# Transposed token buffers laid out by batch, with the third token tile as two 64-column stationary operands

## The chip, the cores and the metric

The kernel runs on one core of one Trainium2 chip. Its time is device microseconds of that core: before the change 1238.06 us, the median of 3 runs (1237.32 to 1239.3). The engines are PE (TensorE, with its weight loads shown as PEld), DVE (VectorE), ACT (ScalarE), POOL (GpSimd) and SP (SyncE, which issues most of the DMAs). They run side by side and meet at semaphores only.

## The reference, cut to what matters

Sixteen images of 112 x 112 become 49 image tokens each (convolutions and a wavelet branch, then a layer norm); a class token is put ahead and 128 text tokens behind, so each batch entry has T = 178 tokens of width D = 192. Then come an attention layer over 12 heads of 16, and a layer with a second attention (its logits are normalised) and a mixture of 4 experts:

```python
h = concat([tok(x), txt], axis=1)                        # (16, 178, 192)
h = h + attn(layernorm(h), w_qkv, b_qkv, scale, w_proj, b_proj)   # diagonal of the non-class part masked
# ffn(layernorm(h)), added to h:
logits = gamma * zscore_last(q @ k.T * hd ** -0.5)
x = layernorm(src + softmax(logits) @ v @ Wo.T + bo)
gate_scores = softmax(x @ Wg.T + bg)                     # 4 experts, the two best are kept
h1 = relu(einsum('btd,edf->ebtf', x, W1) + b1)           # 192 -> 768, for each expert
y = einsum('ebtf,efd->ebtd', h1, W2) + b2                # 768 -> 192
out = layernorm(x + einsum('ebtd,bte->btd', y, combine))
```

## The kernel before, in words

After a stage that makes the image tokens (up to about 160 us), the batch is worked off in 8 pairs of two entries, 356 tokens a pair. With **tokens in the partitions** a pair has three tiles of 128 rows: the text of entry 0, the text of entry 1, and a third tile whose rows 0 to 49 are the image and class tokens of entry 0 and rows 64 to 113 those of entry 1. With **tokens in the columns** (the transposed buffers `xT`, `x2T_hi`, `x2T_lo`, `osb`, `oT`, `hid` and their PSUM banks) a buffer has XW = 384 columns in the same order: 128 of text, 128 of text, 64 of images, 64 of images. So a tile is always one run of 128 columns (`tile_cols`, L593), and whoever works through all tokens takes XN = 370 columns, of which 356 hold tokens.

Each pair goes through attention twice (s = 0 and 1) and then through the experts. A round of the program handles three pairs at a time: the first attention of pair a, the second of pair b, the experts of pair m. Everything is ordered by hand: each engine has its own program, and the expert work is cut into 50 steps a pair which are put between the attention's steps by the tables FILL, FILL_A7 and FILL_B7 (so many steps at each named point). Even steps are `MoePe.step` of unit u (24 units: 4 experts x 6 slices of 128): five matmuls with w1 stationary and the tokens moving (L655), which split a float32 product into float32r parts. Odd steps are `second` (L677): the slice's hidden values `hid` are stationary, one 128-column tile at a time, and w2's 192 columns move. So on PE L655 and L677 take turns. The first rounds have no expert work; there `pe_warm` (L751) puts dummy matmuls between. The last round has expert work alone.

What else the change touches on PE: `pe_project` (L776) makes queries and keys for all tokens at once; `pe_tokens` (L784) makes values and output projections, with each tile of tokens stationary; `pe_out` (L879) turns the attention's result `osb` back, three 128 x 128 transposes for each tile; `bias` (L665) adds the experts' biases with `combT` stationary; the gate's scores (L999) are four small matmuls a tile. The logits (`pe_logits`, L811, L817, L826) aren't changed, but L817 already works with halves of 64 columns that land in the upper and lower partitions, and so does L503 in the image stage.

On ACT the copies of queries, keys, `mrows` and `osb` (L1054 to L1098) are each two instructions, one for the text columns and one for the image columns, since their destination is ordered by batch. On DVE `dve_front1` centres the tokens in two pieces, and `dve_gate` (L1392, L1393) adds up the gate's scores.

Of the kernel before, what the change touches and what calls it, by code (L numbers as in the profile page):

```python
# [29 lines left out]
ALU = mybir.AluOpType  # L30
ACT = mybir.ActivationFunctionType
# [3 lines left out]
HC = D // 2  # L35
# [25 lines left out]
XN = 2 * NTXT + 64 + NB  # L61
# [23 lines left out]
CHAIN_STEPS = {"dve_tok": 15, "dve_front0": 19, "dve_front1": 10, "dve_norm1": 13, "dve_split": 8, "dve_max0": 8, "dve_max1": 8,  # L85
# [50 lines left out]
def build(nc, a):  # L136
    ctx = ExitStack()
    with ctx:
# [391 lines left out]
        xbar = sb("xbar", [HC, 2, 2, 2])  # L530
# [54 lines left out]
        def text(t):  # L585

            return t[:, :, 0:2 * NTXT].rearrange("p h (b j) -> p h b j", b=2)

        def images(t, n=NB):

            return t[:, :, 2 * NTXT:XW].rearrange("p h (b j) -> p h b j", b=2)[:, :, :, 0:n]

        def tile_cols(t, half, i):  # L593

            return t[:, half, 128 * i:128 * i + 128]
# [37 lines left out]
        class MoePe(Moe):  # L633


            def step(self, u, odd):
# [6 lines left out]
                elif u == UNITS:  # L643
                    pe.wait_ge(S["comb_ready"], at(m, 1, 1))
                    for i in range(3):
                        ins = nc.tensor.transpose(PS[0:E, 4, 128 * i:128 * i + 128], comb[:, i, :], ident[:])
                    ins.then_inc(S["ct_psum"], 1)
                    self.second(UNITS - 1)
                else:
# [9 lines left out]
            def bias(self):  # L659
# [4 lines left out]
                for i in range(3):  # L664
                    ins = nc.tensor.matmul(tile_psum((6, 7), i), combT[:, 128 * i:128 * i + 128], b2[:],  # L665
                                           start=(i != 1), stop=True, skip_group_check=True)
                ins.then_inc(S["bias_psum"], 1)

            def second(self, u):
# [5 lines left out]
                for i in range(3):  # L675

                    ins = nc.tensor.matmul(tile_psum((6, 7), i), hid[u % 2][:, 128 * i:128 * i + 128], w2[:, u, :],  # L677
                                           start=(j == 0 and i != 1), stop=(j == FT - 1), skip_group_check=True)
                ins.then_inc(S["h_used"], 1)

        class MoeAct(Moe):


            def step(self, u, odd):
                act, m = self.eng, self.m
                if not odd and u < UNITS:
# [3 lines left out]
                    nc.scalar.activation(hid[u % 2][:, 0:XN], PS[:, 4 + u % 2, 0:XN], ACT.Relu,  # L690
                                         bias=b1[:, u:u + 1]).then_inc(S["h_ready"], 1)
                elif not odd:
                    act.wait_ge(S["ct_psum"], at(m, 1, 1))
                    nc.scalar.copy(combT[:, 0:XN], PS[0:E, 4, 0:XN]).then_inc(S["ct_ready"], 1)
# [68 lines left out]
        def pe_turn_in(pe, s, r):  # L763

            pe.wait_ge(S["xn_ready", s], at(r, 1, 1))
            for h in range(2):
                for i in range(3):
                    ins = nc.tensor.transpose(PS[0:HC, front(s, r)[h], 128 * i:128 * i + 128], xn[s][:, i, HC * h:HC * h + HC],
# [3 lines left out]
        def pe_project(pe, banks, w, x, done):  # L772

            for m in range(2):
                for k in range(2):
                    ins = nc.tensor.matmul(PS[0:HC, banks[m], 0:XN], w_at[:, w, k, HC * m:HC * m + HC], x[:, k, 0:XN],  # L776
# [3 lines left out]
        def pe_tokens(banks, w, x, done):  # L780

            for i in range(3):
                for k in range(2):
# [994 lines left out]
```

## Time and profile before

| | us |
|---|---|
| median of 3 runs | 1238.06 |
| the profiled execution | 1242.59 |
| its span | 1240.8 |
| PE busy | 1114.1 (90%) |
| PE weight loads busy | 816.6 (66%) |
| DVE busy | 680.4 (55%) |
| ACT busy | 397.6 (32%) |
| mean granted TensorE clock | 0.94 |

Busy time of PE is from modelled ends of matmuls that overlap, so the start of one matmul to the start of the next is the surer measure of what one costs. A float32 matmul is two instructions in the profile. A row of the timeline joins like instructions that follow one another: the number behind x is how many, the second column is the time from the first one's start to the last one's end.

### The profile page before, as it was taken

The numbers are of one execution on the slowest core, as the hardware profiler recorded it, in microseconds if no ns is written. First come the engines' busy times: TensorE is split into PE (matmuls) and PEld (weight loads), VectorE is DVE, ScalarE is ACT, GpSimd is POOL, SyncE is SP. The second block draws the span as 40 slices with busy tenths as digits, with TensorE's granted clock in tenths as the row PEclk, the third lists the DMA queues.
The fourth block names the chain that finished last, engine by engine and source line by source line (L and its number), as shares of the span: only waits on it lengthen the run. The fifth ranks groups of instructions, "written<-read, shape, count | busy, mean of one in ns | idle before, by whom it ended". The sixth has DMA issues, their size and how long they took to land.

```text
span 1240.8 us, 19314 instructions
## 1 busy us (share of the span) xinstructions
PE 1114.1 (90%) x7726; PEld 816.6 (66%) x7726; DVE 680.4 (55%) x1874; ACT 397.6 (32%) x905; POOL 55.6 (4%) x90
## 2 busy tenths in 40 slices
PE   7898887898889999999999999999999989888895
PEld 4343354554577678667866785688578757676795
DVE  3357777454555566556646564665557653643432
ACT  1223221322323343324243334334343333232321
POOL 6001110000000000000000000000000000000000
PEclk9898897999989899989998999899999998898998
DMA  9000034412042104310530152024203320040000
GB/s 307 1 1 0 1 125 82 88 43 46 8 86 66 29 5 106 63 18 10 111 63 9 28 111 45 9 49 90 45 9 73 66 45 2 1 88 8 1 10 9
DMA packets 38481, 60.79 MB, mean 49 GB/s; under 512 B 5060, under 2 KB 30264, under 8 KB 37944
## 3 DMA queue, kind: packets, MB, share of 16 engines
q1 hardware_dynamic: 36112, 56.84, 21.4%
q10 hardware_dynamic: 2280, 2.72, 0.8%
q8 instruction: 61, 1.00, 0.3%
q14 instruction: 28, 0.23, 0.1%
HBM read 42.76 MB, written 16.34 MB: 48 GB/s over the span
## 4 chain that ended last, share of the span: by engine, by line
PE 62%; DVE 15%; ACT 4%; DMA 3%; issue 2%; SPq 1%; POOL 0%; DVEq 0%; ACTq 0%; POOLq 0%
PE PS L677 15%; PE PS L655 12%; DVE mx L1349 7%; PE PS L776 6%; PE PS L870 5%; PE PS L811 5%; PE PS L784 5%; PE PS L817 3%; PE PS L879 2%; PE PS L826 2%; DMA qst<-mrows 1%; PE PS L908 1%; PE PS L999 1%; DVE acc L705 1%; ACT probs L1087 1%
## 5 line engine op out<-in xcount | busy, mean ns | idle before, releaser
L677 PE MATMUL PS<-w,hid 128*128 128x192 f32 x1152 | 233.1, 340 | 2.6 <-DVE acc L705 1.9
L690 ACT ACTIVATE hid<-PS,b 128x370 f32<-128x370 f32 x192 | 109.3, 569 | 321.7 <-PE PS L655 320.1
L677 PEld LDWEIGHTS PS<-w,hid 128*128 128x128 f32 x1152 | 199.1, 198 | 13.5 <-issue 4.8
L1349 DVE TENSOR_REDUCE mx<-PS 128x2 f32<-128x356 f32 x288 | 128.8, 521 | 130.8 <-PE PS L811 100.6
L1087 ACT ACTIVATE probs<-PS 128x356 f32<-128x356 f32 x288 | 110.8, 484 | 21.9 <-PE PS L811 12.4
L655 PE MATMUL PS<-x2T_hi,w_hi 128*128 128x370 f32 x192 | 91.2, 475 | 0.0
L811 PE MATMUL PS<-kst,qst 96*128 96x178 bf16 x384 | 66.6, 269 | 12.8 <-DMA kst<-scr_k 5.5
L826 PE MATMUL PS<-masks,ident_bf 128*128 128x256 bf16 (+1 forms) x288 | 75.4, 262 | 0.0
L870 PE MATMUL PS<-probs,va 128*17 128x178 f32 x1536 | 67.3, 315 | 6.4 <-ACT probs L1087 6.4
L776 PE MATMUL PS<-xT,w_at 96*96 96x370 f32 x192 | 67.1, 493 | 2.9 <-ACT xT L1047 2.0
L655 PE MATMUL PS<-x2T_lo,w_hi 128*128 128x370 f32 x192 | 66.0, 344 | 0.0
L655 PE MATMUL PS<-x2T_hi,w_lo 128*128 128x370 f32 x192 | 65.9, 343 | 0.0
L655 PE MATMUL PS<-x2T_hi,w_rest 128*128 128x370 f32 x192 | 65.8, 343 | 0.0
L655 PE MATMUL PS<-x2T_lo,w_rest 128*128 128x370 f32 x192 | 65.7, 342 | 0.0
L811 PE MATMUL PS<-qst,kst 99*128 99x178 bf16 x384 | 54.5, 243 | 9.7 <-DMA qst<-mrows 6.1
L751 PE MATMUL PS<-masks,ident_bf 128*128 128x356 bf16 x322 | 57.0, 324 | 4.0 <-POOL hid L1674 4.0
L1370 DVE RECIPROCAL rs<-PS 128x36 f32<-128x36 f32 x16 | 6.1, 383 | 97.5 <-PE PS L879 97.5
L811 PEld LDWEIGHTS PS<-kst,qst 96*128 96x128 bf16 x384 | 26.4, 103 | 44.4 <-DVE mx L1349 28.3
L870 PEld LDWEIGHTS PS<-probs,va 128*17 128x17 f32 x1536 | 39.9, 97 | 22.6 <-ACT probs L1087 9.2
L384 DVE SCALAR_TENSOR_TENSOR dwo<-pad_l,chan,dwo 96x441 f32<-96x441 f32 x48 | 38.0, 792 | 27.5 <-ACT cw L308 26.0
L776 PEld LDWEIGHTS PS<-xT,w_at 96*96 96x96 f32 x192 | 30.7, 167 | 30.6 <-ACT xT L1047 5.6
L705 DVE SCALAR_TENSOR_TENSOR acc<-PS,comb,acc 128x192 f32<-128x192 f32 x72 | 25.6, 411 | 43.0 <-PE PS L677 43.0
(228 smaller groups left out, 1760.9 us busy)
## 6 DMA issues: line engine op xcount, KB each, us to landing
qst<-scr_q SPq DMA_DIRECT2D x96, 144.0 KB, 4.8
scr_q<-qs SPq DMA_DIRECT2D x16, 432.0 KB, 3.3
scr_k<-ks SPq DMA_DIRECT2D x16, 432.0 KB, 3.3
kst<-scr_k SPq DMA_DIRECT2D x16, 432.0 KB, 5.0
kst<-scr_k SPq DMA_DIRECT2D x16, 288.0 KB, 5.9
cols<-in_x_cols SPq DMA_DIRECT2D x6, 392.0 KB, 10.0
w<-in_w SPq DMA_DIRECT2D x1, 2304.0 KB, 26.2
kst<-scr_k SPq DMA_DIRECT2D x16, 144.0 KB, 6.3
```

The lines of the kernel that those rows point to most:

```text
L655: ins = nc.tensor.matmul(PS[:, 4 + u % 2, 0:XN], w[:, f], x[:, plane, 0:XN], start=(k == 0), stop=(k == 4))
L677: ins = nc.tensor.matmul(tile_psum((6, 7), i), hid[u % 2][:, 128 * i:128 * i + 128], w2[:, u, :], start=(j == 0 and i != 1), stop=(j == FT ...
L690: nc.scalar.activation(hid[u % 2][:, 0:XN], PS[:, 4 + u % 2, 0:XN], ACT.Relu, bias=b1[:, u:u + 1]).then_inc(S["h_ready"], 1)
L705: ins = nc.vector.scalar_tensor_tensor(out=acc[:, i, :], in0=tile_psum((6, 7), i), scalar=comb[:, i, e:e + 1], in1=(acc if e else x2)[:, i ...
L751: nc.tensor.matmul(PS[:, 7, 0:T2], ident_bf[:], masks[:], start=True, stop=True)
L776: ins = nc.tensor.matmul(PS[0:HC, banks[m], 0:XN], w_at[:, w, k, HC * m:HC * m + HC], x[:, k, 0:XN], start=(k == 0), stop=(k == 1))
L784: ins = nc.tensor.matmul(tile_psum(banks, i), tile_cols(x, k, i), w_at[:, w, k, :], start=(k == 0), stop=(k == 1))
L811: ins = nc.tensor.matmul(PS[:, bank, T * b:T * b + T], still[0:rows_, h, TP * b:TP * b + NTXT], move[0:rows_, h, TP * b:TP * b + T], start ...
L826: ins = nc.tensor.matmul(own, ident_bf[:], m.rearrange("p (b j) -> p b j", b=2), start=False, stop=True, skip_group_check=True)
L870: ins = nc.tensor.matmul(PS[32 * q:32 * q + VW, 3, T * b:T * b + T], va[s][:, 2 * i + b, h, :], pr, start=(i == 0), stop=(i == 1), skip_gr ...
L1087: nc.scalar.activation(probs[:, u % PROB_UNITS, bank, :], PS[:, bank, 0:T2], ACT.Exp)\
L1349: nc.vector.tensor_reduce(out, PS[:, g, 0:T2].rearrange("p (b j) -> p b j", b=2), AX.X, ALU.max)\
```

## The change

All buffers with tokens in the columns now hold 192 columns for each of the two entries: 128 of text, 50 of images and class, 14 unused. Work on all tokens takes 2 x 178 = 356 columns in two runs (`by_batch`). The two text tiles are still 128 columns in one run, but the third tile is 64 columns at 128 and 64 columns at 320. As a moving operand or as output of a transpose that is one access of 2 x 64 (`tile_of`). As a stationary operand it is two (`lhs_of`), each of 64 columns, whose results go to partitions 0 to 63 and 64 to 127.

```diff
-XN = 2 * NTXT + 64 + NB
+GATE_COLS = (0, 192, 128, 256)
...
+        def by_batch(t, n=T):
+            return t.rearrange("p (b j) -> p b j", b=2)[:, :, 0:n]
...
+        def lhs_of(t, i):
+            if i < 2:
+                return ((t[:, TP * i:TP * i + NTXT], slice(0, 128)),)
+            return tuple((t[:, TP * b + NTXT:TP * b + TP], slice(64 * b, 64 * b + 64)) for b in range(2))
...
-                        ins = nc.tensor.matmul(PS[:, 4 + u % 2, 0:XN], w[:, f], x[:, plane, 0:XN],
+                        ins = nc.tensor.matmul(by_batch(PS[:, 4 + u % 2, 0:XW]), w[:, f], by_batch(x[:, plane, :]),
                                                start=(k == 0), stop=(k == 4))
...
                 for i in range(3):
-                    ins = nc.tensor.matmul(tile_psum((6, 7), i), hid[u % 2][:, 128 * i:128 * i + 128], w2[:, u, :],
-                                           start=(j == 0 and i != 1), stop=(j == FT - 1), skip_group_check=True)
+                    for lhs, rows_ in lhs_of(hid[u % 2][:], i):
+                        ins = nc.tensor.matmul(tile_psum((6, 7), i)[rows_], lhs, w2[:, u, :],
+                                               start=(j == 0 and i != 1), stop=(j == FT - 1), skip_group_check=True)
...
         def pe_tokens(banks, w, x, done):
             for i in range(3):
-                for k in range(2):
-                    ins = nc.tensor.matmul(tile_psum(banks, i), tile_cols(x, k, i), w_at[:, w, k, :],
-                                           start=(k == 0), stop=(k == 1))
+                for half in range(1 if i < 2 else 2):
+                    for k in range(2):
+                        lhs, rows_ = lhs_of(x[:, k, :], i)[half]
+                        ins = nc.tensor.matmul(tile_psum(banks, i)[rows_], lhs, w_at[:, w, k, :],
+                                               start=(k == 0), stop=(k == 1), skip_group_check=True)
...
                 for g in range(3):
-                    ins = nc.tensor.transpose(PS[:, i, 128 * g:128 * g + 128], osb[:, g, 128 * i:128 * i + 128], ident[:])
+                    for lhs, rows_ in lhs_of(osb[:, g, :], i):
+                        ins = nc.tensor.matmul(PS[rows_, i, 128 * g:128 * g + 128], lhs, ident[:], start=True, stop=True,
+                                               skip_group_check=True)
...
-                for i in range(3):
+                for i, lo in enumerate(GATE_COLS):
                     o = 2 * E * i
...
-                for src, c in zip(by_token(front(s, r)[h]), (slice(0, NTXT), slice(NTXT, T))):
...
+                src, out = by_batch(PS[0:HC, front(s, r)[h], 0:XW]), q32[s][:, h, :, 0:T]
...
-            nc.scalar.copy(osb[:, g, 0:2 * NTXT].rearrange("p (b j) -> p b j", b=2), o[:, :, 0:NTXT])
-            nc.scalar.copy(osb[:, g, 2 * NTXT:XW].rearrange("p (b j) -> p b j", b=2)[:, :, 0:NB], o[:, :, NTXT:T])\
-                .then_inc(S["o_ready", s], 1)
+            nc.scalar.copy(by_batch(osb[:, g, :]), o).then_inc(S["o_ready", s], 1)
...
-            ch.link(nc.vector.tensor_tensor(gl[:], parts[:, :, 0], bg[:].unsqueeze(1).to_broadcast([128, 3, E]), ALU.add))
-            nc.vector.tensor_tensor(gl[:], parts[:, :, 1], gl[:], ALU.add).then_inc(S["gate_used"], 1)
+            nc.vector.tensor_tensor(gl[:, 0:2], parts[:, 0:2, 0], bg[:].unsqueeze(1).to_broadcast([128, 2, E]), ALU.add)
+            for b_ in range(2):
+                p = slice(64 * b_, 64 * b_ + 64)
+                ins = nc.vector.tensor_tensor(gl[p, 2], parts[p, 2 + b_, 0], bg[p], ALU.add)
+            ch.link(ins)
...
```

`bias` (L665) goes through `lhs_of` in the same way, and the transposes to tokens-in-columns (L768, L844, L885, L986) write through `tile_of`. The copies of `k32`, `mrows` and `combT` and the centring in `dve_front1` lose their split into text and images. The tables FILL, FILL_A7 and FILL_B7 stay as they are.

On PE, where a round of attention ends and expert steps follow, the rows before are these (L870 is the probabilities times values, L879 `pe_out`; the shape is that of the result, and the number behind x counts whole matmuls):

```order
L870 MATMUL PS<-probs,va 17x178 x16
L879 MATMUL PS<-ident,osb 128x128 x9
L655 MATMUL PS<-x2T_hi,w_hi 128x370
L655 MATMUL PS<-x2T_hi,w_lo 128x370
L655 MATMUL PS<-x2T_lo,w_hi 128x370
L655 MATMUL PS<-x2T_hi,w_rest 128x370
L655 MATMUL PS<-x2T_lo,w_rest 128x370
L677 MATMUL PS<-w,hid 128x192 x3
```

The same place on PE after the change, where L887 is `pe_out`, L658 is the step of w1 and L682 is `second`:

```order
L877 MATMUL PS<-probs,va 17x178 x16
L887 MATMUL PS<-ident,osb 128x128 x6
L887 MATMUL PS<-ident,osb 64x128 x6
L658 MATMUL PS<-x2T_hi,w_hi 128x2x178
L658 MATMUL PS<-x2T_hi,w_lo 128x2x178
L658 MATMUL PS<-x2T_lo,w_hi 128x2x178
L658 MATMUL PS<-x2T_hi,w_rest 128x2x178
L658 MATMUL PS<-x2T_lo,w_rest 128x2x178
L682 MATMUL PS<-w,hid 128x192 x2
L682 MATMUL PS<-w,hid 64x192 x2
```

No instruction changes its place. The nine of L879 become twelve, six of them with 64 stationary columns, and the three of L677 become four, two of them with 64.

On DVE, where the gate's scores come out of PSUM (`dve_gate`; `va` is the last step of the values ahead of it), before:

```order
L1231 TENSOR_TENSOR va<-PS,rows 50x12x16 x2
L1392 TENSOR_TENSOR gl<-PS,bg 128x12
L1393 TENSOR_TENSOR gl<-PS,gl 128x12
L1395 TENSOR_REDUCE gs<-gl 128x3
L1396 TENSOR_TENSOR gl<-gl,gs 128x12
```

and after:

```order
L1228 TENSOR_TENSOR va<-PS,rows 50x12x16 x2
L1387 TENSOR_TENSOR gl<-PS,bg 128x8
L1390 TENSOR_TENSOR gl<-PS,bg 64x4 x2
L1392 TENSOR_TENSOR gl<-PS,gl 128x8
L1395 TENSOR_TENSOR gl<-PS,gl 64x4 x2
L1398 TENSOR_REDUCE gs<-gl 128x3
L1399 TENSOR_TENSOR gl<-gl,gs 128x12
```

Two instructions have become six; those behind them stand in the same order.

## Rows read from the trace of the kernel before

**Rows 1.** Page, busy time: us, share of the span, instructions.
```profile
PE 1114.1 (90%) x7726; PEld 816.6 (66%) x7726; DVE 680.4 (55%) x1874; ACT 397.6 (32%) x905; POOL 55.6 (4%) x90
```

**Rows 2.** Page, chain that ended last: shares of the span.
```profile
PE 62%; DVE 15%; ACT 4%; DMA 3%; issue 2%; SPq 1%; POOL 0%; DVEq 0%; ACTq 0%; POOLq 0%
PE PS L677 15%; PE PS L655 12%; DVE mx L1349 7%; PE PS L776 6%; PE PS L870 5%; PE PS L811 5%; PE PS L784 5%; PE PS L817 3%; PE PS L879 2%; PE PS L826 2%; DMA qst<-mrows 1%; PE PS L908 1%; PE PS L999 1%; DVE acc L705 1%; ACT probs L1087 1%
```

**Rows 3.** Chain in order of time, last round: start us, us, piece.
```profile
1184.47 0.98 PE PS L677 x6
1185.45 0.84 PE PS L655 x5
```

**Rows 4.** Timeline, PE, around the halves of L817: start us, us, line, count.
```profile
436.85 0.24 PE L811 MATMUL PS<-qst,kst 99*128 99x178 bf16 x1
437.02 0.34 PE L817 MATMUL PS<-qst,kst 99*64 99x178 bf16 x4
...
437.29 0.59 PE L677 MATMUL PS<-w,hid 128*128 128x192 f32 x2
...
437.56 0.49 PE L677 MATMUL PS<-w,hid 128*128 128x192 f32 x2
...
438.37 0.47 PE L811 MATMUL PS<-qst,kst 99*128 99x178 bf16 x4
```

**Rows 5.** Timeline, into the float32 halves of L503.
```profile
152.65 1.15 PE L458 MATMUL PS<-pad_l,diag 96*96 96x392 f32 x3
153.73 2.71 PE L503 MATMUL PS<-w_pw,flat 96*64 96x192 f32 x30
...
153.31 0.49 PE L458 MATMUL PS<-pad_l,diag 96*96 96x392 f32 x1
...
153.94 0.50 PE L503 MATMUL PS<-w_pw,flat 96*64 96x192 f32 x4
```

**Rows 6.** Chain in order of time: start us, us, piece.
```profile
1052.76 0.98 PE PS L879 x9
...
596.02 1.47 PE PS L999 x12
```

**Rows 7.** Timeline behind the gate of one round.
```profile
597.53 0.17 DVE L1392 TENSOR_TENSOR gl<-PS,bg 128x12 f32<-128x12 f32 x1 [0.37 <-PE PS L999]
...
598.50 0.57 ACT L690 ACTIVATE hid<-PS,b 128x370 f32<-128x370 f32 x1
...
599.17 0.55 PE L677 MATMUL PS<-w,hid 128*128 128x192 f32 x2
```

**Rows 8.** Timeline and chain, where PE waits behind expert steps.
```profile
637.80 0.49 PE L844 MATMUL PS<-ident,mpart 128*36 128x128 f32 x3 [1.00 <-DVE mpart L1358]
...
642.66 0.31 PE L811 MATMUL PS<-qst,kst 99*128 99x178 bf16 x2 [0.70 <-DMA qst<-mrows]
...
1117.66 2.48 issue
```

**Rows 9.** Groups by form: count, busy us, mean ns, idle before.
```profile
L776 PE MATMUL PS<-xT,w_at 96*96 96x370 f32 x192 | 67.1, 493 | 2.9 <-ACT xT L1047 2.0 <-ACT q L1054 0.8
L920 PE MATMUL PS<-rem,same_head 96*96 96x356 f32 x32 | 11.5, 482 | 1.9 <-DVE rem L1329 1.2
...
L1097 ACT COPY osb<-PS 128x256 f32<-128x256 f32 x48 | 17.9, 373 | 49.8 <-PE PS L870 49.8
L1098 ACT COPY osb<-PS 128x100 f32<-128x100 f32 x48 | 11.9, 249 | 0.0
```

**Rows 10.** Timeline: PE behind ACT in the first attention's exponentials.
```profile
652.57 1.40 PE L870 MATMUL PS<-probs,va 128*17 128x178 f32 x32 [0.67 <-ACT probs L1087]
```

**Rows 11.** Stretches: us, then busy of PE, PEld, DVE, ACT, POOL, clock, DMA.
```profile
628.00:635.00 7.00, 7.00 (x62) 3.44 (x61) 7.00 (x17) 1.29 (x3) 0.00 (x0) 1.00 0.01 2
654.00:657.50 3.50, 2.69 (x25) 1.08 (x25) 3.23 (x8) 0.52 (x2) 0.00 (x0) 0.99 0.00 0
657.60:664.20 6.60, 6.60 (x33) 4.03 (x32) 6.29 (x21) 0.00 (x0) 0.00 (x0) 0.50 0.01 2
```

More of the change, by code:

```diff
@@ L664, in bias @@
                 for i in range(3):
-                    ins = nc.tensor.matmul(tile_psum((6, 7), i), combT[:, 128 * i:128 * i + 128], b2[:],
-                                           start=(i != 1), stop=True, skip_group_check=True)
+                    for lhs, rows_ in lhs_of(combT, i):
+                        ins = nc.tensor.matmul(tile_psum((6, 7), i)[rows_], lhs, b2[:],
+                                               start=(i != 1), stop=True, skip_group_check=True)
                 ins.then_inc(S["bias_psum"], 1)
@@ L689, in step @@
                         act.wait_ge(S["h_used"], at(m, UNITS, u - 1))
-                    nc.scalar.activation(hid[u % 2][:, 0:XN], PS[:, 4 + u % 2, 0:XN], ACT.Relu,
+                    nc.scalar.activation(by_batch(hid[u % 2][:]), by_batch(PS[:, 4 + u % 2, 0:XW]), ACT.Relu,
                                          bias=b1[:, u:u + 1]).then_inc(S["h_ready"], 1)
@@ L1065, in act_key @@
             for h in range(2):
-                for src, c in zip(by_token(front(s, r)[h]), (slice(0, NTXT), slice(NTXT, T))):
-                    if s == 0:
-                        ins = nc.scalar.activation(k32[:, h, :, c], src, ACT.Identity, bias=chan[:, C_BK + h:C_BK + h + 1])
-                    else:
-                        ins = nc.scalar.copy(k32[:, h, :, c], src)
+                src, out = by_batch(PS[0:HC, front(s, r)[h], 0:XW]), k32[:, h, :, 0:T]
+                if s == 0:
+                    ins = nc.scalar.activation(out, src, ACT.Identity, bias=chan[:, C_BK + h:C_BK + h + 1])
+                else:
+                    ins = nc.scalar.copy(out, src)
             ins.then_inc(S["k_f32", s], 1)
@@ L1075, in act_max_rows @@
             act.wait_ge(S["mT_psum", s], at(r, 1, 1))
[L1076 to L1079 removed]
+            nc.scalar.copy(mrows[:], PS[0:3 * HEADS, 3, 0:XW]).then_inc(S["m_rows", s], 1)
         def act_exp_pass(act, s, r, moe):
@@ L1390, in dve_gate @@
             dve.wait_ge(S["gate_psum"], at(b, 1, 1))
-            parts = PS[:, 2, 0:6 * E].rearrange("p (i c e) -> p i c e", c=2, e=E)
-            ch.link(nc.vector.tensor_tensor(gl[:], parts[:, :, 0], bg[:].unsqueeze(1).to_broadcast([128, 3, E]), ALU.add))
-            nc.vector.tensor_tensor(gl[:], parts[:, :, 1], gl[:], ALU.add).then_inc(S["gate_used"], 1)
+            parts = PS[:, 2, 0:8 * E].rearrange("p (i c e) -> p i c e", c=2, e=E)
+            nc.vector.tensor_tensor(gl[:, 0:2], parts[:, 0:2, 0], bg[:].unsqueeze(1).to_broadcast([128, 2, E]), ALU.add)
[3 more added lines that the diff above has]
+            ch.link(ins)
+            nc.vector.tensor_tensor(gl[:, 0:2], parts[:, 0:2, 1], gl[:, 0:2], ALU.add)
+            for b_ in range(2):
+                p = slice(64 * b_, 64 * b_ + 64)
+                ins = nc.vector.tensor_tensor(gl[p, 2], parts[p, 2 + b_, 1], gl[p, 2], ALU.add)
+            ins.then_inc(S["gate_used"], 1)
             dve.wait_ge(S["gate_used"], at(b, 1, 1))
```

67 lines of the change are left out of this document (27 added, 40 removed).

## The prediction, made before the changed kernel ran

> **What bounds the kernel now.** I read the busy times first: PE is busy for 90% of the span, DVE for 55%, ACT for 32% [rows 1]. Busy PE alone proves little, so I read the chain that ended last: 62% of the span is PE work, first L677 and L655, the two halves of an expert step, and 15% is DVE, most of it the maxima of L1349 [rows 2]. The chain in order of time shows how dense the expert work is: in the last round six instructions of L677 take 0.98 us and five of L655 take 0.84 us, with nothing between, so a unit takes 1.82 us and there are 24 a pair [rows 3]. What PE gains or loses in these steps is nearly all gained or lost at the end. The timeline then shows where PE waits behind expert steps, which could hide something: 1.00 us for the maxima, 0.70 us for a DMA, and 2.48 us once in the last round of attention [rows 8].
>
> **What a third tile in two halves costs.** Two things have to be known: whether two halves of 64 columns run side by side, and what going into and out of them costs.
>
> Side by side: L503 is the same case, float32 halves whose results go to the lower and the upper partitions, with 192 columns moving, in the order two or four of the one half, then of the other. Thirty of them take 2.71 us, 0.082 us each after the first 0.33, where L677 with the same moving columns takes 0.98/6 = 0.163 us each [rows 3, 5]. So two run abreast, and the eight instructions of four whole matmuls take as long as six did: the halves themselves cost nothing.
>
> Into the halves: L458 takes 0.33 us each, (1.15 - 0.49)/2, but the first L503 starts 0.42 us after the last L458: 0.09 us more. The second slot of L503 starts 0.21 us after the first, not 0.16: 0.05 us more, a load that isn't hidden [rows 5]. The bfloat16 case has the same step: L817 starts 0.17 us after the last L811, whose own spacing is (0.47 - 0.24)/3 = 0.077 us [rows 4].
>
> Out of them: the last of four L817 starts at 437.02 + 0.34 - 0.24 = 437.12 and L677 at 437.29, 0.17 us later instead of 0.077: 0.095 us. Then two L677 take 0.59 us where the next two take 0.49 us: 0.10 us, again an open load [rows 4]. In all 0.09 + 0.05 + 0.095 + 0.10 = 0.34 us for one third tile. As a lower bound I keep the two stops without the loads, 0.19 us; as an upper bound 0.34 plus the 0.33 us of halves that don't run abreast.
>
> The Trainium skill has a rule here that speaks against the change (TensorEngine Tiling (Array Packing), Key Properties): changing the tiling mode, not just the tile, drains the engine. The trace agrees, with 0.09 us on each side; the page has no price. Another page (TensorE: Matmul & The Clock Gate, Step-by-step: what each phase is for) says that the queue pulls the next weight load ahead of running matmuls; the 0.59 against 0.49 us behind L817 speaks against that across such a border.
>
> How many: 192 in `second`, 32 in `pe_tokens` (values and output, twice a pair), 16 in `pe_out`, 8 in `bias`, 248 in all; none is beside another, since other 128-column work stands between (L655 behind L677). 248 x 0.34 = 84.3 us.
>
> **The other parts on PE that add.** `pe_out`: nine transposes take 0.98 us, 0.109 each [rows 6]. As plain float32 matmuls they are two instructions each (L677 has 0.163 us for 192 columns, so 0.109 for 128). Six whole ones take 12 x 0.109 = 1.31, six halves two abreast 6 x 0.109 = 0.65, together 1.96: 0.98 us more, 16 times, 15.7 us. It is on the path, since DVE's `rs` waits for its last. The gate's fourth tile: twelve matmuls take 1.47 us [rows 6], so four more take about 0.48, 8 times, 3.8 us.
>
> **DVE at the gate.** Four more small instructions of nearly 0.17 us each [rows 7], 0.66 us. Behind them stands ACT's exponential, and behind that, in ACT's queue, the first `hid`, which ends at 598.50 + 0.57 = 599.07; the L677 that needs it starts at 599.17 [rows 7]. The cover is 0.10 us, so about 0.55 us is seen, in perhaps 6 of 8 rounds: 3.3 us. In the others something else is later; both ends, 0 and 8 x 0.66, stay in the range.
>
> **What is hidden.** In a full round the third tile before the L844 that waits 1.00 us for the maxima, and the two before the L811 that waits 0.70 us for a DMA, cost nothing [rows 8]: 3 x 0.34, just inside the waits. With six such rounds that is 6.1 us. In the last attention round 2.48 us stand open behind eight units, and a few more at the later waits: 3.9 us. Together 10.0 us off. The DVE-bound passes of maxima have no expert steps in the full rounds, so they hide nothing.
>
> **What is saved.** L655 has 356 columns instead of 370: 14/370 of 0.84/5 = 0.168 us is 0.0064, 960 times, 6.1 us, of which 0.5 is hidden: 5.6. Queries and keys: L776 with 370 columns has a mean of 493 ns, L920 with 356 in two runs 482 [rows 9]; 0.011 us over 256 instructions is 2.8 us. This pair also says that two runs of 178 move no slower than one run. ACT: two copies of `osb` take 0.373 + 0.249 us; the slope between them is 0.0008 us a column, so one of 356 columns takes 0.45, 0.17 less [rows 9]. It counts where PE waits for ACT: at the end of each pass (16 x 0.17 = 2.7), twice in each first-attention pass, where L870 waits 0.67 us for `probs` [rows 10] (2.7), and about 0.15 for `mrows` in eight rounds (1.2): 6.6 us. The other merged copies, the shorter centring on DVE and the narrower `hid` lie beside PE work; without that cover they would give back some 0.3 us a copy. Transposes with a 2 x 64 output move the same 128 columns: nothing, with a tenth of a us a round either way as bounds.
>
> **The sum.** 84.3 + 15.7 + 3.8 + 3.3 - 10.0 - 5.6 - 2.8 - 6.6 = 82.1 us. The profiled execution took 1242.6 us (span 1240.8 and 1.8 around it), so its like would take 1324.7. The median of the runs is 4.5 us lower, at 1238.1: **1320 us**.
>
> **Rivals.**
> 1. *The next load is pulled ahead, only the stop remains.* A third tile then costs 0.19 instead of 0.34 us, 37 us less: **1283 us**. For it: float32 halves have longer loads, and none of their exits to L655 is in the trace. Against it: both open loads in [rows 4, 5]. 12%. (The Trainium skill's sentence on loads pulled ahead would lead here.)
> 2. *The granted clock falls more often.* It was 0.50, the 1.2 GHz level, in 657.6 to 664.2, right after a stretch in which PE was busy 2.69 of 3.50 us and stood waiting for DVE; it was 1.00 in 628 to 635, with PE waiting on DVE less [rows 11]. The stops leave PE streaming for about 1.8 of each 2.1 us, denser than either, which speaks against it. One more stretch of 6.6 us at half clock in each of seven rounds costs 7 x 3.3 = 23 us: **1343 us**. 9%.
> 3. *The halves run one after the other.* Where two instructions of one half stand before two of the other, the queue might not mix them. 192 x 0.33 + 32 x 0.65 + 16 x 0.65 + 8 x 0.33 = 97 us more: **1417 us**. L503 speaks against it [rows 5]. 4%.
> 4. *The other side: the waits take it all up.* PE is idle for 127 us of the span; if its idle time stood behind the added work everywhere, only ACT's and DVE's savings would be seen, 1238 - 7 = **1231 us**. The place is each wait behind an expert step; it decides once the waits there are longer than the 0.34 us of every third tile. For it: that idle time is as large as the addition. Against: in the last round 24 units in a row have none at all [rows 3], and in a full round only three of 24 have a wait behind them. 3%.
>
> **How the numbers follow.** The forecast has 70%, with its own range 1300 to 1338 (0.30 to 0.40 us a third tile, the gate's chain between its ends). The four rivals take 28%, and 2% is for a mixture that ends near the old time. A change of less than 0.2%, 2.5 us, can't be told from none by this measurement. Slower: 0.70 + 0.12 + 0.09 + 0.04 = 0.95; faster 0.03; same 0.02. The range takes in the first two rivals: 1282 to 1345 us.
>
> **What the profile will show.** In the last round a unit takes 1.82 + 0.34 - 0.03 = 2.13 us, and the first 64-column instruction of `second` starts 0.09 us late; behind the halves the next two starts are about 0.17 and 0.27 us apart. `pe_out` takes 2.3 us instead of 0.98. PE still holds most of the chain. The waits of L844 and of the L811 behind the DMA shrink from 1.00 and 0.70 to some 0.7 and 0.2 us. L655 starts every 0.165 us. I am wrong if the exit from the halves shows no open load (then rival 1), if halves start 0.16 us apart instead of together (rival 3), or if the end moves by much less than the sum over PE.

## The result, and the profile after

The changed kernel took 1325.91 us (median of 4 runs, 1320.76 to 1336.14). The kernel before, run beside it, took 1238.68 us (4 runs, 1237.32 to 1239.6). The ratio is 1.0711, 95% interval 1.0665 to 1.0757: 87 us slower, where 82 were forecast. The profiled execution took 1322.18 us. Below, a median is of all runs, and a ratio leaves out runs of more than 1.5% above the fastest of their kernel (one in experiment 4, two each in experiments 5 and 8).

The page of the kernel after, busy times and chain, against [rows 1, 2]:

```profile
PE 1204.1 (91%) x8526; PEld 801.7 (61%) x8526; DVE 682.4 (52%) x1882; ACT 381.4 (29%) x777; POOL 56.3 (4%) x90
PE 66%; DVE 14%; ACT 4%; issue 2%; DMA 2%; SPq 0%; POOL 0%; DVEq 0%; POOLq 0%; ACTq 0%
PE PS L682 17%; PE PS L658 13%; DVE mx L1344 7%; PE PS L791 5%; PE PS L781 5%; PE PS L877 5%; PE PS L818 4%; PE PS L887 3%; PE PS L824 3%; PE PS L1008 2%; PE PS L833 2%; PE PS L917 1%; ACT probs L1086 1%; DVE acc L710 1%; PE PS L894 1%
```

PE is busy for 90 us more and the span is 80 us longer. The addition is on PE, whose share of the chain rose from 62% to 66%. DVE is where it was; ACT is busy for 16 us less, but the span didn't get shorter by that.

The chain in order of time, last round, against [rows 3]:

```profile
1270.65 1.13 PE PS L682 x8
1271.77 1.02 PE PS L658 x5
```

A unit takes 2.15 us where it took 1.82. L658 reads 1.02 instead of 0.84, although it has 14 columns less: the chain counts from the end of the piece ahead, so L658 carries the way out of the halves. (A border here means one way into the 64-column halves and one way out.) The starts show how this comes about. The timeline of PE in three narrow windows (start us, us, line, shape, count):

```profile
1270.97 0.33 PE L682 MATMUL PS<-w,hid 128*128 128x192 f32 x1
...
1271.23 0.38 PE L682 MATMUL PS<-w,hid 128*64 128x192 f32 x2
...
1271.70 0.43 PE L658 MATMUL PS<-x2T_hi,w_hi 128*128 128x356 f32 x1
...
1271.97 0.33 PE L658 MATMUL PS<-x2T_hi,w_lo 128*128 128x356 f32 x1
1272.14 0.32 PE L658 MATMUL PS<-x2T_lo,w_hi 128*128 128x356 f32 x1
```

The first 64-column instruction starts 0.26 us after the last one of 128 instead of 0.16, and both halves start together (x2 within 0.38 us, their starts are 7 ns apart). L658 follows 0.47 us later, and its second 0.27 us after that, where the next ones keep 0.165. To the ns of the trace, each against the usual start distance: 0.093 us more at the entry, 0.051 at the second pair of halves, 0.093 at the exit, 0.106 for the open load behind it, 0.343 us in all.

The other places on PE (chain in order of time; `pe_out`, the biases, the gate's scores in a round at full and in one at half clock):

```profile
715.68 2.38 PE PS L887 x24
...
742.21 1.38 PE PS L669 x8
...
615.75 1.88 PE PS L1008 x16
...
748.16 3.50 PE PS L1008 x16
```

And what PE waited for, in all, before and after (us in total, times, longest us):

```profile
PE PS L844 <- DVE mpart L1358: 7.9, 8, 1.2
PE PS L870 <- ACT probs L1087: 6.4, 9, 1.0
PE PS L811 <- DMA qst<-mrows: 6.1, 8, 1.0
PE PS L811 <- DMA kst<-scr_k: 5.5, 1, 5.5
PE PS L879 <- ACT osb L1098: 5.1, 7, 0.7
PE PS L879 <- ACT mrows L1078: 4.7, 7, 0.7
PE PS L811 <- issue: 2.5, 1, 2.5
```

```profile
PE PS L877 <- ACT probs L1086: 5.8, 9, 1.0
PE PS L851 <- DVE mpart L1353: 5.7, 8, 0.8
PE PS L818 <- DMA kst<-scr_k: 5.1, 1, 5.1
PE PS L887 <- ACT osb L1096: 4.7, 7, 0.7
PE PS L887 <- ACT mrows L1078: 4.2, 7, 0.7
...
PE PS L818 <- DMA qst<-mrows: 1.8, 2, 1.0
```

Behind expert steps the waits shrank by 2.2 us (maxima), 4.3 (DMA), 0.4 (`kst`), and the 2.48 us of [rows 8] are gone: 9.4 us of the addition were hidden, 10.0 were forecast. The 0.4 is scatter more than effect: between experiments 9 and 10 the same wait went from 5.1 to 5.5 us. The waits for ACT that the forecast named shrank by 0.6 + 0.4 + 0.5 = 1.5 us, where 6.6 were forecast. Those for the copies of queries and keys, which it took as covered, shrank by another 1.8 us.

The granted clock falls more often. Stretches at half clock (0.50, the level of 1.2 GHz), added up over the clock records from 170 us on, are 116 us before and 139 after. The new ones lie around the gate, behind the biases and the transposes of x, in the five rounds with full work (from 478, 611, 745, 878 and 1011 us on). The kernel before has such a stretch in the first of these rounds alone, 3.4 us from 469.7 on. Windows of the kernel after (us, busy of PE, PEld, DVE, ACT, POOL, clock, DMA):

```profile
478.20:481.80 3.60, 3.60 (x18) 2.88 (x16) 1.23 (x3) 0.80 (x1) 0.00 (x0) 0.52 0.95 177
...
744.60:754.80 10.20, 10.20 (x42) 9.06 (x41) 4.60 (x19) 1.40 (x3) 0.00 (x0) 0.50 0.73 148
```

Ahead of the second, PE had stood idle for 1.2 us on DVE's `acc`, as in every round of both kernels. Values, scores and two steps of w1 then run at half speed: the scores take 3.50 instead of 1.88 us.

### The profile page after: what moved, and what is told of

Read it like the earlier page. It is cut to its first block, busy times and chain, and to the rows that moved or that the text cites. A ratio compares the mean times of both kernels' runs of the same rounds, so it can differ in the third digit from the quotient of the medians.

```text
span 1320.4 us, 20794 instructions
## 1 busy us (share of the span) xinstructions
PE 1204.1 (91%) x8526; PEld 801.7 (61%) x8526; DVE 682.4 (52%) x1882; ACT 381.4 (29%) x777; POOL 56.3 (4%) x90
## 4 chain that ended last, share of the span: by engine, by line
PE 66%; DVE 14%; ACT 4%; issue 2%; DMA 2%; SPq 0%; POOL 0%; DVEq 0%; POOLq 0%; ACTq 0%
PE PS L682 17%; PE PS L658 13%; DVE mx L1344 7%; PE PS L791 5%; PE PS L781 5%; PE PS L877 5%; PE PS L818 4%; PE PS L887 3%; PE PS L824 3%; PE PS L1008 2%; PE PS L833 2%; PE PS L917 1%; ACT probs L1086 1%; DVE acc L710 1%; PE PS L894 1%
## 5 line engine op out<-in xcount | busy, mean ns | idle before, releaser
L682 PE MATMUL PS<-w,hid 128*128 128x192 f32 (+1 forms) x1536 | 261.1, 350 | 1.8 <-DVE acc L710 1.2
L695 ACT ACTIVATE hid<-PS,b 128x356 f32<-128x356 f32 x192 | 106.8, 556 | 376.8 <-PE PS L658 375.6
L682 PEld LDWEIGHTS PS<-w,hid 128*128 128x128 f32 (+1 forms) x1536 | 171.4, 167 | 58.1 <-issue 50.3
L658 PE MATMUL PS<-x2T_hi,w_hi 128*128 128x356 f32 x192 | 87.9, 458 | 0.0
L833 PE MATMUL PS<-masks,ident_bf 128*128 128x256 bf16 (+1 forms) x288 | 75.5, 263 | 0.0
L781 PE MATMUL PS<-xT,w_at 96*96 96x356 f32 x192 | 65.6, 486 | 2.3 <-ACT xT L1051 2.0
L658 PE MATMUL PS<-x2T_hi,w_lo 128*128 128x356 f32 x192 | 66.4, 346 | 0.0
L658 PE MATMUL PS<-x2T_lo,w_hi 128*128 128x356 f32 x192 | 66.0, 344 | 0.0
L658 PE MATMUL PS<-x2T_hi,w_rest 128*128 128x356 f32 x192 | 66.0, 344 | 0.0
L658 PE MATMUL PS<-x2T_lo,w_rest 128*128 128x356 f32 x192 | 65.4, 341 | 0.0
L658 PEld LDWEIGHTS PS<-x2T_hi,w_hi 128*128 128x128 f32 x192 | 38.4, 200 | 38.6 <-issue 34.3
```

Of the source, the lines that this page charges most:

```text
L658: ins = nc.tensor.matmul(by_batch(PS[:, 4 + u % 2, 0:XW]), w[:, f], by_batch(x[:, plane, :]), start=(k == 0), stop=(k == 4))
L682: ins = nc.tensor.matmul(tile_psum((6, 7), i)[rows_], lhs, w2[:, u, :], start=(j == 0 and i != 1), stop=(j == FT - 1), skip_group_check=True)
L695: nc.scalar.activation(by_batch(hid[u % 2][:]), by_batch(PS[:, 4 + u % 2, 0:XW]), ACT.Relu, bias=b1[:, u:u + 1]).then_inc(S["h_ready"], 1)
L781: ins = nc.tensor.matmul(by_batch(PS[0:HC, banks[m], 0:XW]), w_at[:, w, k, HC * m:HC * m + HC], by_batch(x[:, k, :]), start=(k == 0), stop ...
L833: ins = nc.tensor.matmul(own, ident_bf[:], m.rearrange("p (b j) -> p b j", b=2), start=False, stop=True, skip_group_check=True)
```

## The experiments

All ratios are to the kernel before, run beside them: 1237.96 us beside experiments 1 to 4 (11 runs), 1238.11 us beside 5 to 8 (16 runs), 1236.84 us beside 9 to 12 (17 runs). A difference of two of these medians is uncertain by some 6 to 9 us, by the intervals of the ratios.

**1. The halves of `second` undone.** Largest term by itself.

```diff
-                    for lhs, rows_ in lhs_of(hid[u % 2][:], i):
-                        ins = nc.tensor.matmul(tile_psum((6, 7), i)[rows_], lhs, w2[:, u, :], ...
+                    ins = nc.tensor.matmul(tile_psum((6, 7), i), hid[u % 2][:, 128 * i:128 * i + 128], w2[:, u, :], ...
...
-                    nc.scalar.activation(by_batch(hid[u % 2][:]), by_batch(PS[:, 4 + u % 2, 0:XW]), ACT.Relu, ...
+                    src = by_batch(PS[:, 4 + u % 2, 0:XW])
+                    nc.scalar.activation(hid[u % 2][:, 0:256].rearrange("p (b j) -> p b j", b=2), src[:, :, 0:NTXT], ACT.Relu, ...
+                    nc.scalar.activation(hid[u % 2][:, 256:XW].rearrange("p (b j) -> p b j", b=2)[:, :, 0:NB], ...
```

> The changed kernel with one part undone: hid is again in the order of tiles (ACT writes it in two instructions, text and images), and second works with three stationary operands of 128 columns; everything else stays changed. Theory A (each way into and out of 64-column halves costs a fixed 0.34 us): 192 such places go, some 25 of them hidden, so about -55 us, 1326 to 1270; a unit in the last round takes 0.98 + 0.81 = 1.80 us instead of 2.15. Theory B (a good part of the 87 us is the granted clock, which falls a second time in each round since PE streams less densely): the second stretch at half clock in each round goes too, another -10 us or so, 1260. Theory C (the cost is in the narrower w1 step, whose columns now come in two runs, not in the halves): hardly any change, above 1310.

Measured: 1276.81 us (4 runs), ratio 1.0332 (1.0278 to 1.0385), 49 us less than the changed kernel. Its chain in the last round, and two starts of PE one unit apart:

```profile
1219.76 0.98 PE PS L681 x6
...
1225.00 1.14 PE L681 MATMUL PS<-w,hid 128*128 128x192 f32 x6
...
1226.80 1.14 PE L681 MATMUL PS<-w,hid 128*128 128x192 f32 x6
```

A unit takes 1.80 us, 0.35 less than 2.15, so the 0.34 of a border is there. The kernel gave back 49 us: more than half the cost is here, but 192 x 0.34 would be 65. Experiment 11 measures the same at a steadier clock. The stretches at half clock around the gate stayed, 157 us in all, more than the 139 of the changed kernel. So theory B is refuted: the halves of `second` don't call for them. Theory C is out too.

**2. `pe_out` undone** (three transposes a tile again, `osb` by tile, written in two instructions).

```diff
-                    for lhs, rows_ in lhs_of(osb[:, g, :], i):
-                        ins = nc.tensor.matmul(PS[rows_, i, 128 * g:128 * g + 128], lhs, ident[:], start=True, stop=True, ...
+                    ins = nc.tensor.transpose(PS[:, i, 128 * g:128 * g + 128], osb[:, g, 128 * i:128 * i + 128], ident[:])
```

> The changed kernel with pe_out undone: osb in the order of tiles, two ACT copies for each group, nine transposes of 128 x 128. Theory A: per turn 0.98 us of further matmuls and 0.34 us of border go, 16 times, -21 us, and the split ACT copies give back some 4: 1326 to 1309. If DVE or ACT set the pace around pe_out, less than half of that. Theory B makes no difference here, unless the second stretch at half clock goes.

Measured: 1302.56 us (4 runs), ratio 1.0539 (1.0488 to 1.0589), 23 us less. The forecast's terms for it are 15.7 + 16 x 0.34 = 21.1, less some 4 for the split ACT copies that come back with it; 23 agrees with them within the scatter.

**3. The biases' halves undone** (`combT` by tile).

```diff
-                    for lhs, rows_ in lhs_of(combT, i):
-                        ins = nc.tensor.matmul(tile_psum((6, 7), i)[rows_], lhs, b2[:], ...
+                    ins = nc.tensor.matmul(tile_psum((6, 7), i), combT[:, 128 * i:128 * i + 128], b2[:], ...
```

> The changed kernel with bias undone: combT in the order of tiles, three matmuls of 128 stationary columns. Theory A: 8 borders, -2.7 us, 1323. Theory B, if the border in bias, right after the wait for DVE's acc, is what tips the clock: the stretch at half clock that begins near the next gate in rounds 3 to 7 goes, -2.7 and about -15 more, 1308, with a mean granted clock of 0.95 instead of 0.93.

Measured: 1328.75 us (6 runs), ratio 1.0736 (1.0701 to 1.0771): no less than the changed kernel, with a mean clock of 0.928 in the profiled run. The new stretches stayed in all five rounds, so that the halves of the biases make the clock fall is refuted. The 2.7 us of theory A are too few to be seen in such a difference.

**4. All tiles of `second` in halves.** The text tiles too are two accesses of 64 columns, so there is no border inside `second`.

```diff
-                    for lhs, rows_ in lhs_of(hid[u % 2][:], i):
+                    h_ = hid[u % 2]
+                    lo = (TP * i, TP * i + 64) if i < 2 else (NTXT, TP + NTXT)
+                    for b_ in range(2):
+                        lhs, rows_ = h_[:, lo[b_]:lo[b_] + 64], slice(64 * b_, 64 * b_ + 64)
```

> The changed kernel with the text tiles of second in halves of 64 columns too: six stationary operands, two abreast, so 12 float32 instructions instead of 8, and still one way in and one way out of the 64-column form for each unit. Theory A (the border costs, halves by themselves nothing): no change, 1326 within the scatter of the clock, and a unit of the last round takes 2.15 us. Theory D (it is the number of instructions or of weight loads that costs): 4 more instructions a unit, half as many again as the change added, +20 to +50 us.

Measured: 1314.13 us (4 runs), ratio 1.0592 (1.0536 to 1.0649). Its chain in the last round:

```profile
1273.56 1.02 PE PS L658 x5
1274.59 1.13 PE PS L685 x12
1275.71 1.02 PE PS L658 x5
```

Twelve instructions of 64 columns take the 1.13 us of the eight, and the unit stays at 2.15: halves run abreast, and the price is of going in and out, wherever the border lies. Theory D, a price for each instruction or load, is out. The kernel is even 12 us below the changed one (with wide runs, 1304 to 1324). At some 22 places `second` follows the 64-column logits (L824 in the changed kernel, L827 here); there the trace has a start distance of 0.073 us at full clock instead of 0.170. That accounts for about 22 x 0.2 us at most; the rest isn't settled.

**5. Halves in the values alone.** All other stationary halves undone: the edits of experiments 1 to 3, and for the output projection these.

```diff
+                    ins = nc.tensor.transpose(PS[0:HC, h, 128 * i:128 * i + 128], on[:, i, HC * h:HC * h + HC], ident[:])
...
+                    ins = nc.tensor.matmul(tile_psum((2, 3), i), oT[:, k, 128 * i:128 * i + 128], w_at[:, 4 * s + 3, k, :], ...
```

> The changed kernel with all halves undone but those of the values: hid, osb, oT and combT are in the order of tiles and 128 columns stationary again; the narrower w1 step and projections, the merged copies of queries, keys and mrows, the gate's fourth tile and the halves in the 16 value steps stay. Theory A, as a sum of parts: before -6 (w1) -3 (projections) -1 to -3 (ACT) +5.5 (16 borders) +4 (gate's matmuls) +3 (DVE at the gate), so 1238 +- 5: the halves were all that mattered. If the parts don't add up, for instance because the clock falls a second time in each round whatever second does, 1255 or more.

Measured: 1264.41 us (6 runs), ratio 1.0139 (1.0079 to 1.0199). The expectation was 1238. The median missed it by 26 us; the four runs that the ratio uses (1247 to 1265) have a median of 1260, 22 above it. The profiled run (1265.1) has the lowest mean clock of all profiles, 0.919, with 173 us at half clock against before's 116; stretches of 6.8 to 13.7 us in a round lie around the gate in all five rounds. Half of the 57 us more would be 29 us, about the miss. So the borders aren't all that costs time. That the rest is the clock is argued from this count; no run has this kernel with the clock held up.

**6. The gate's part alone, in the kernel before** (four tiles of scores, six DVE additions for two).

```diff
-                for i in range(3):
+                for i, t_ in enumerate((0, 1, 2, 2)):
...
-            nc.vector.tensor_tensor(gl[:], parts[:, :, 1], gl[:], ALU.add).then_inc(S["gate_used"], 1)
+            nc.vector.tensor_tensor(gl[:, 0:2], parts[:, 0:2, 1], gl[:, 0:2], ALU.add)
+            for b_ in range(2):
+                p = slice(64 * b_, 64 * b_ + 64)
+                ins = nc.vector.tensor_tensor(gl[p, 2], parts[p, 2 + b_, 1], gl[p, 2], ALU.add)
```

> The kernel before with the gate's part alone: four tiles of scores (the third twice) and six DVE additions instead of two, with the same result. Theory A: 8 x (0.48 on PE + 0.55 of the chain DVE, ACT, hid) = +4 to +8 us, 1242 to 1246. If DVE's additions are hidden: +2 to +4.

Measured: 1255.55 us (6 runs), ratio 1.0136 (1.0095 to 1.0177): 17 us for a part that the forecast has at 7.1. A window of it, columns as above:

```profile
707.00:722.00 15.00, 14.83 (x57) 14.42 (x58) 6.10 (x25) 2.15 (x4) 0.00 (x0) 0.54 0.81 146
```

Such a stretch appears around the gate of two rounds (708 to 722 us, and 3.4 us at 592), with none of the new halves in the kernel. So they aren't needed for it. The time at half clock is 143 us in all, against 116. What in the order of the work tips the clock, no run here isolates.

**7. Dummy matmuls ahead of the biases' wait**, in the changed kernel. Their result is never read. PE stands idle there for 1.2 us a round.

```diff
             def bias(self):
+                for _ in range(7):
+                    nc.tensor.matmul(PS[:, 5, 0:T2], ident_bf[:], masks[:], start=True, stop=True)
```

> The changed kernel with seven dummy matmuls of 356 columns (about 1.05 us) ahead of PE's wait for acc in bias, where PE stands idle for about 1.3 us just ahead of the second stretch at half clock. Theory B (that wait, close to the borders, lets the clock fall once more in each round): the second stretch goes, some 6 rounds x 3 to 5 us, 1326 to 1300. Rival (the wait has nothing to do with it): 1326, no change, or up to 2 us slower where the dummies outlast the wait.

Measured: 1308.60 us (4 runs), ratio 1.0579 (1.0534 to 1.0624), clock 0.948: 17 us less than the changed kernel, where some 26 were expected. The stretches around the gate are gone in all five rounds, and 108 us at half clock are left of 139: half of the 31 us is about what came back. The window at the place of 744.60 above:

```profile
735.60:745.20 9.60, 9.33 (x65) 7.50 (x66) 5.66 (x23) 1.91 (x4) 0.00 (x0) 1.00 0.70 122
```

**8. Dummy matmuls in the maxima**, in the kernel before: two of 156 columns behind each bank of logits of the second attention, where PE waits for DVE.

```diff
                 ins.then_inc(filled, 1)
+                if keep_busy:
+                    for _ in range(2):
+                        nc.tensor.matmul(PS[:, 3, T2:512], ident_bf[:], masks[:, 0:512 - T2], start=True, stop=True)
...
+                if busy and u == 1 and free is not None:
+                    pe.wait_ge(S["o_ready", 0], at(free, 3, 3))
```

The dummies write into bank 3, which ACT still reads for the first attention's result, so the second unit waits for `o_ready` first and the dummies start with it.

> The kernel before with two dummy matmuls of 156 columns (0.13 us) behind each bank of the second attention's maxima (from its second unit on), where PE stands idle for about 0.27 us a bank while DVE takes the maxima, and behind which the granted clock falls to half in each round for 6.8 us. Theory B (PE's waits there make it fall): the stretch goes in 6 or 7 rounds, 3.4 us each, 1238 to 1216. Rival (the dummies change nothing in the clock, or only move the fall): 1238 to 1242.

Measured: 1232.79 us (12 runs), ratio 0.9952 (0.9923 to 0.9981). The stretches behind the maxima (in the kernel before from 538, 657, 777 and 896 us on) are gone, with 78 us at half clock instead of 116. But the kernel gained 5 us where 22 were expected; half of the time that is no longer at half clock would be 19. Time at half clock can't be halved to give its price at every place: here most of it didn't come back. Part of it became waiting: ahead of L850 (L844 in the kernel before) PE now waits 7.5 us for the maxima and 6.0 with no releaser shown, against 7.9 and 0.6. The rest isn't settled, and the added wait for `o_ready` could be in it. The place of the third window of [rows 11], in the kernel before and then with the dummies:

```profile
650.00:664.50 14.50, 13.02 (x125) 7.48 (x118) 9.92 (x29) 2.16 (x8) 0.00 (x0) 0.76 0.10 14
```

```profile
650.00:664.50 14.50, 12.99 (x114) 9.92 (x115) 11.01 (x31) 2.03 (x5) 0.00 (x0) 1.00 0.02 4
```

With both sets the clock can be held up in both kernels, all but alike, and the change be priced there. The last four experiments have both; "held clock" below means this.

**9. The kernel before with both sets.**

> The kernel before with both sets of dummy matmuls: two of 156 columns behind each bank of logits in the second attention's maxima, and seven of 356 columns ahead of the wait of bias. Theory (what the granted clock takes is taken behind waits of PE, and work put into the waits gives it back): the half-clock stretch behind the maxima is gone as with the first set alone, and nothing else changes, since before had no second half-clock stretch behind the biases: 1228 to 1236 us. Rival (dummies ahead of a wait delay what stands behind them, since they aren't all covered): 7 x 0.16 us, 8 times, up to 9 us over the kernel with the first set alone, 1240 to 1246.

Measured: 1227.26 us (7 runs), ratio 0.9926 (0.9901 to 0.9952), clock 0.964. This is the version that beats both kernels; its first set stands in `bias` as in 7, its second as in 8. The rival, dummies that aren't covered by the wait and cost up to 9 us, is out.

**10. The changed kernel with both sets.**

> The changed kernel with both sets of dummy matmuls. Theory (of the 87 us that the change costs, some 12 to 15 are the lower granted clock; the borders and pe_out are the rest): 70 to 78 us over the kernel before with both sets, about 1300 to 1308, with a granted clock near that kernel's. Rival (the clock has nothing to do with the sum, the borders cost all of it): 82 to 88 us over it.

Measured: 1302.74 us (5 runs), ratio 1.0537 (1.0498 to 1.0575), clock 0.963. Against experiment 9 the change costs 75.5 us; without the dummies 87.2. So some 12 us of the loss are the clock, an uncertain figure as a difference of two differences. The count supports it: time at half clock is 57 us in experiment 9 and 62 here, 5 us apart instead of 23, and half of those 18 us is 9. The hold isn't perfect: three stretches of 3.4 us are left around the gate (at 486, 616 and 1002 us). The clock line of the page (40 slices of the span), of the changed kernel and of this one:

```profile
PEclk9898897999898989898989898989898999799898
```

```profile
PEclk9898897999899999999999999999999999799998
```

**11. The changed kernel with both sets and without the halves of `second`.** The edits of 1, 7 and 8.

> The changed kernel with the halves of second undone (its three tiles are 128 columns in one run again, hid written by two ACT instructions), with both sets of dummy matmuls. Sizes the largest term by itself at a clock that is kept up. By the forecast's term, 192 third tiles at 0.34 us less those hidden by waits, it takes 55 to 65 us off the changed kernel with both sets. Theory (some 22 of the 192 follow other work of 64 columns and have no border, and waits hide more than the forecast took): 48 to 54 us off. Rival (the borders cost 0.19, the clock the rest): 30 to 36 us off.

Measured: 1255.31 us (5 runs), ratio 1.0154 (1.0113 to 1.0195): 47 us for the halves of `second` at a held clock, by the intervals some 40 to 54. The forecast's term, 55 to 65 us, is too large, and the rival of 30 to 36 (0.19 a border) is out. PE waits for `hid` 1.1 us more here than in experiment 10, since ACT writes it in two instructions, as neither kernel does; so the halves cost about 1 us more than the 47.

**12. The gate's part alone with both sets.** The edits of 6, 7 and 8.

> The gate's part of the change alone (four tiles of scores, six small DVE additions for two), with both sets of dummy matmuls. The same part without them cost 17 us, where 4 to 8 were forecast. Theory (the part itself is cheap, and the rest was a second half-clock stretch behind it in each round): with the clock kept up it costs 3 to 8 us over the kernel before with both sets. Rival (the gate's chain is on the path in every round, and costs 2 us a round whatever the clock does): 15 to 18 us over it.

Measured: 1236.59 us (11 runs, 1231.79 to 1240.56), 9 us over experiment 9 (1224.35 to 1229.44), and by the two traces 7 us behind the image stage. That is at the upper end of the 3 to 8 us of the theory; the rival of 15 to 18 us, a gate that costs 2 us a round at any clock, is out. So of the 17 us of experiment 6 some 8 are the clock.

## Why the prediction was right, point by point

The size and the mechanism came out: 1325.9 against 1320, nearly all of it work and stops that PE adds. But terms of the sum were off on both sides.

**A border in and out.** Forecast 0.09 + 0.05 + 0.095 + 0.10; found 0.093 + 0.051 + 0.093 + 0.106. The halves run abreast, and both loads are open (not hidden behind other work). This is shown by the rows after and by experiments 1 and 4. Rival 1 is out: the load isn't pulled ahead. Rival 3 is out: 7 ns between the halves.

**How many at the full price, mis-sized.** The forecast took 0.34 us at all 248 places. A border costs that only where plain 128-column work follows. I matched experiments 9 and 10 place by place, from the start of `second` to the second start behind it. Before the w1 step it took 0.343 us more (107 places). Before queries and keys, which have 96 stationary columns, it was 0.243 on the mean, between 0.15 and 0.31 (12). Between 64-column logits and the next logits it was 0.253 (11), and before probabilities times values, with 17 columns, 0.15 (7). The last of these in rows, from experiment 10 and then experiment 9 (timeline of PE):

```profile
579.88 0.55 PE L684 MATMUL PS<-w,hid 128*64 128x192 f32 x4
580.36 0.65 PE L885 MATMUL PS<-probs,va 128*17 128x178 f32 x12
```

```profile
555.89 0.81 PE L679 MATMUL PS<-w,hid 128*128 128x192 f32 x4
556.63 0.65 PE L878 MATMUL PS<-probs,va 128*17 128x178 f32 x12
```

The last of L684 starts at 579.88 + 0.55 - 0.33 = 580.10, the last of L679 at 555.89 + 0.81 - 0.33 = 556.37, and the next one 0.26 us later in both: the 17-column work paid its own entry before the change, and pays no more now. Where I could match them (174 places) the sum is 54 us, 0.31 each. Less the 9.4 us that waits hid, some 50 are left for all 192, and experiment 11 measured 47, or 48 with the wait for `hid`.

**`pe_out`.** Forecast 1.96 us at full clock, and 2.3 with the border; found 2.38. In all 23 us against 21. Right.

**Values, biases and scores, a little over-sized.** At a held clock the values took 2.11 instead of 1.95 us, the biases 1.38 instead of 1.24; the exit is in the step behind. The gate's scores took 1.89 instead of 1.47, 0.42 more with that exit in it. Values and scores together are 0.58 us more a round, where 0.34 + 0.48 = 0.82 were forecast. This is to be seen in the chains of experiment 10 and then 9, of one round each:

```profile
740.63 2.11 PE PS L793 x16
742.74 1.89 PE PS L1016 x16
...
746.65 1.39 PE PS L684 x8
```

```profile
822.42 1.95 PE PS L786 x12
824.37 0.09 issue
824.46 1.47 PE PS L1007 x12
825.93 1.84 PE PS L655 x10
```

**DVE at the gate, over-sized.** These rows show it on the path as forecast: from the end of the scores to `second` 746.65 - (742.74 + 1.89) = 2.02 us, where it was 1.84. That is 0.18 us a round instead of 0.55, or 0.24 without the 0.06 that the ten narrower matmuls of w1 in between save. Between the scores and `second` PE has these ten matmuls to do, which cover most of the chain. Where the clock falls there nothing is seen, since they then take 3.2 us. The size of the whole part is settled by experiment 12: 7 to 9 us against 7.1.

**Hidden.** 9.4 us against 10.0, by the waits named: L851 waits 0.7 us a round, and the DMA's wait is nearly gone. In experiment 1 both are back, with 8.2 and 6.1 us in all.

**The narrower w1 step, right.** In the traces of experiments 9 and 10 its inner start distances are 0.172 and 0.166 us, 0.006 less as forecast; the unit of experiment 1 takes 1.80 us where it took 1.82.

**ACT's merged copies, mis-sized.** 1.5 us against 6.6. The group of the kernel after, by form, beside [rows 9]:

```profile
L1096 ACT COPY osb<-PS 128x356 f32<-128x356 f32 x48 | 21.9, 456 | 52.2 <-PE PS L877 52.2
```

The copy takes 0.456 us as worked out, and 0.373 + 0.249 - 0.456 is 0.17. But the two copies don't follow end to end. The chains of experiment 9 and then 10, between values-by-probabilities and `pe_out`:

```profile
677.26 0.03 ACT osb L1105
677.28 0.24 issue
677.52 0.26 ACT osb L1106
```

```profile
711.31 0.47 ACT osb L1104
```

The two take 677.52 + 0.26 - 677.26 = 0.52 us together, the one 0.46 to 0.47: 0.06 saved at most, not 0.17. The second began 0.10 us before the end of the first, as it does in all 48 pairs. The step that failed is the sum of two busy times. Queries and keys have 486 ns a matmul where they had 493, 0.007 less and not 0.011: 1.8 us for 2.8.

**The clock.** Rival 2 had 9% and 23 us. It happened, beside the forecast and not in its place: stretches at half clock around the gate in each of five rounds, where the kernel before has one, some 12 us in all by experiments 9 and 10. The argument against it, that PE streams more densely, looked at the expert steps; the stretches begin elsewhere, behind the biases' wait for DVE. Dummy work in that wait ends them (experiment 7), and so they hang on it. The new halves aren't needed for them: undoing those of `second` or of the biases left them (experiments 1 and 3), and the gate's part alone brought them in two rounds (experiment 6). Why the same wait of 1.2 us leaves the clock up in most rounds of the kernel before and not in the changed one, or in experiments 5 and 6, isn't settled: no run moved the wait alone.

**Rival 4** is out: PE's waits were as large as the addition, but 9.4 us of them took anything up.

So the sum of 82.1 stood 6.6 us above the 75.5 that the change costs at a held clock, which by the intervals lies between 70 and 81. The savings of ACT and the projections were too large by 5.1 + 1.0, so the costs must have been too large by some 12.7: 6 of them are the exits of `second` (65.3 against 192 x 0.31), and 2 are the values and scores (8 x 0.24). The other 5 us (3, if the waits for queries and keys count as saved) are within the scatter, and no run settles them. The clock put 12 on top of the 75.5, which the forecast had as a rival and not in its sum. That the forecast came within 6 us of the median is therefore partly luck: one error of 6.6 us too much and one of 12 too little cancelled in part.

## What to carry to other kernels

Count the places where PE goes from 128 stationary columns to 64 and back, not the instructions: here each trip cost 0.34 us beside 0.16 us matmuls, as much for two halves as for six, and less if the work next door pays its own change of shape anyway.

Don't add up busy times to price a merge: two copies with 0.62 us of busy time took 0.52 us, so the merged one of 0.46 us saved 0.06 and not 0.17. And count such a saving only in the waits that it ends.

Before a small difference is explained, hold the clock up in both kernels with dummy matmuls in PE's waits: the same edit read 17 us without them and 9 with them.

## What the runs showed of the hardware that was not expected

Matmuls whose results nobody reads made the kernel before faster: 1227.3 against 1236.8 us. With 2 x 156 columns behind each bank and 7 x 356 columns ahead of one wait the time at half clock went from 116 to 57 us. Of those 59 us 10 came back as time, not half of them; in the changed kernel 31 us less (experiment 7) gave back 17.

A part of 7 to 9 us in the gate cost 17 while the clock was free, and undoing the halves everywhere but in the values left 173 us at half clock, more than either kernel. What the clock takes doesn't go by the amount of work that is added.

With 64-column instructions on both sides (experiment 4 behind L824) the next start came after 0.073 us, where it came after 0.170 with 128 columns behind 64, although L824 is bfloat16 and `second` float32: a change of type alone made no stop here.
